# Perceiver layer on one core: the turned contexts of the cross-attention loop move behind the first score block, into the two value banks

## What is computed

```python
x = x + cross_attention(layernorm(x), ctx_768)      # 64 batches, 32 queries, 257 keys of 384, 16 heads of 64
x = x + self_attention(layernorm(x))                # 16 heads, a bias by relative position
x = x + ffn(layernorm(x))                           # weights and activations rounded to 8 bits; gated, 1408 wide
# cross_attention:
q, k, v = hidden @ Wq, ctx @ Wk, ctx @ Wv           # heads of 64
probs = softmax(q @ k.T / 8)
out = (probs @ v) @ Wo + bo
```

## Time and profile before

| | us |
|---|---|
| median of 3 runs | 1572.41 |
| lowest and highest | 1572.11, 1574.92 |
| the profiled execution, its own time | 1571.98 |
| its span, first to last instruction | 1570.2 |

### The profile page before, as it was taken

One profiled execution on the slowest core, in us unless ns is written; L12 is line 12 of the kernel. 1 busy time (PEld: TensorE's weight loads), 2 busy tenths in 40 slices (PEclk: granted clock), 3 DMA queues, 4 the chain that ended last, 5 costly groups with the idle time before them and its releaser, 6 DMA issues.

```text
span 1570.2 us, 36060 instructions
## 1 busy us (share of the span) xinstructions
PE 1533.9 (98%) x13794; PEld 1286.7 (82%) x13802; DVE 1063.5 (68%) x2274; ACT 736.5 (47%) x1596; POOL 371.4 (24%) x225
## 2 busy tenths in 40 slices
PE   7999989999999999999999999999999999998989
PEld 6888788899999899988989999888888888886544
DVE  8766677677667766677667767657555664556788
ACT  5444655555545554555455554433223222224755
POOL 1000234343444344443534344400000000000000
PEclk9999999999999999999999999999999999999999
DMA  6799863341433233332344143250220311323022
GB/s 239 317 369 355 316 254 126 140 146 52 140 136 141 68 116 139 139 109 75 139 139 144 53 140 124 82 195 29 94 83 29 122 42 42 115 77 128 1 107 107
DMA packets 78958, 210.74 MB, mean 134 GB/s; under 512 B 5712, under 2 KB 31760, under 8 KB 76048
## 3 DMA queue, kind: packets, MB, share of 16 engines
q1 hardware_dynamic: 78864, 209.39, 37.1%
HBM read 140.42 MB, written 68.94 MB: 133 GB/s over the span
## 4 chain that ended last, share of the span: by engine, by line
PE 89%; issue 6%; DVE 3%; ACT 1%; DMA 0%; SPq 0%; POOLq 0%; POOL 0%
PE psum_o L697 17%; PE psum_s L674 8%; PE psum_q L674 8%; PE psum_q L1538 6%; PE psum_o L1494 6%; PE psum_q L1494 6%; PE psum_q L727 6%; PE psum_t L1570 6%; PE psum_o L562 5%; PE psum_o L712 5%; PE psum_t L685 3%; PE psum_t L643 3%; PE psum_t L594 1%; PE psum_q L594 1%; PE psum_s L1525 1%
## 5 line engine op out<-in xcount | busy, mean ns | idle before, releaser
L697 PE MATMUL psum_o<-pT,c_nat 128*128 128x512 f32 x1152 | 307.4, 403 | 3.4 <-issue 2.4
L697 PEld LDWEIGHTS psum_o<-pT,c_nat 128*128 128x128 f32 x1152 | 204.6, 189 | 40.1 <-DVE pT L962 3.6
L1310 POOL TENSOR_TENSOR c_nat<-c_raw,constants 128x768 fp32r<-128x768 f32 x64 | 93.9, 1467 | 555.3 <-PE psum_o L697 440.7
L1163 DVE TENSOR_SCALAR oT<-psum_o,c_last 128x512 f32<-128x512 f32 x192 | 143.8, 749 | 66.5 <-PE psum_o L697 66.5
L889 ACT ACTIVATE probs<-psum_s,nmax 128x257 f32<-128x257 f32 x128 | 61.1, 477 | 233.0 <-DVE nmax L1178 233.0
L674 PE MATMUL psum_s<-cT,qk 128*128 128x256 f32 (+1 forms) x1152 | 163.8, 287 | 0.5 <-DVE cT L962 0.3
L674 PEld LDWEIGHTS psum_s<-cT,qk 128*128 128x128 f32 x1152 | 150.1, 189 | 6.6 <-issue 0.5
L674 PE MATMUL psum_q<-cT,qk 128*128 128x256 f32 (+1 forms) x1152 | 151.7, 283 | 1.0 <-DVE qk L1097 1.0
L674 PEld LDWEIGHTS psum_q<-cT,qk 128*128 128x128 f32 x1152 | 142.2, 189 | 4.0 <-issue 2.6
L962 DVE TENSOR_TENSOR pT<-psum_t,pT 128x512 fp32r<-128x512 f32 x128 | 87.8, 687 | 71.0 <-ACT pT L780 71.0
L1295 POOL TENSOR_TENSOR c_raw<-c_raw,last_row 128x768 f32<-128x768 f32 x64 | 120.3, 1880 | 29.6 <-DMA last_row<-in_ctx_dram 19.2
(11 more groups left out here) (295 smaller groups left out, 3114.5 us busy)
## 6 DMA issues: line engine op xcount, KB each, us to landing
qk_by_tile<-staged SPq DMA_DIRECT2D x32, 1536.0 KB, 10.2
raw<-qk_by_tile SPq DMA_DIRECT2D x16, 3072.0 KB, 12.6
c_raw<-in_ctx_dram SPq DMA_DIRECT2D x64, 384.0 KB, 3.2
last_row<-in_ctx_dram SPq DMA_DIRECT2D x64, 192.0 KB, 4.4
out_dram<-x_out SPq DMA_DIRECT2D x32, 256.0 KB, 2.0
x_res<-in_x_dram SPq DMA_DIRECT2D x16, 256.0 KB, 2.6
x_in<-out_dram SPq DMA_DIRECT2D x4, 1024.0 KB, 7.7
x_all<-out_dram SPq DMA_DIRECT2D x1, 4096.0 KB, 13.4
```

The lines of the kernel that those rows point to most:

```text
L697: i = pe.matmul(ps[:], c_nat[(b - 1) % 2][:, part, k, m * P:(m + 1) * P], pT[:, moving, k, :], start=(k, part, moving) == (0, 0, 0), stop= ...
L1163: nc.vector.tensor_scalar(oT[:, m, :, (b - 1) % 4, :], ps[:].rearrange("p (s q) -> p s q", q=SQ), c_last[:, (b - 1) % 2, m:m + 1], None, A ...
```

## The change

The six context transposes of a batch move from between the value blocks to a place behind S0, in between the probability transposes. The row is now: probabilities half 0 (t0), context chunk 2, probabilities half 1 (t1), context chunks 0 and 1 together. The contexts no longer go through t0 and t1 but through the banks of the coming PV0 and PV1. Chunks 0 and 1 share one bank, so that ScalarE and VectorE drain them with one instruction of 512 columns each. In b = 0 of the first tile all stays as it was. The tests of readiness are the same: probabilities by `s_scaled` and `s_normed`, contexts by `s_sub`. GpSimd's and SyncE's programs are untouched.

```diff
 def cross_units(section):
...
+        later = not (section == "last" and b == 3)
+        if b == 0 and section == "first":
+            u += [(("CT", b, c), ("t0", "t1")[c % 2]) for c in range(3)]
+            continue
+        u += turned_units(b)
+        if later:
+            u += [(("CT", b, 2), values_bank(b, 0)), (("CT", b, 0), values_bank(b, 1))]
         if b == 1 and section != "first":
             u += [(("W", 0), "o1"), (("W", 1), "o0")]
...
+        u += value_units(b)
         if b == 3 and section != "first":
             u.append((("WO",), "q1"))
-        if not (section == "last" and b == 3):
-            u += [(("CT", b, c), ("t0", "t1")[c % 2]) for c in range(3)]
...
         def pe_ctxT(pe, t, b, section, chunks):
 
-            if chunks[0] == 0:
+            if chunks[0] == chunks_of(b, section)[0][0]:
                 pe.wait_ge(s_sub, 4 * t + (b + 2))
-            for c in chunks:
-                pe_ctxT_chunk(pe, U1(("CT", b, c), t, section), c_raw[(b + 1) % 2], c)
+            pe_ctxT_chunk(pe, U1(("CT", b, chunks[0]), t, section), c_raw[(b + 1) % 2], chunks)
...
             for k in range(KI):
-                if k == KI // 2 and section in ("second", "loop"):
-                    pe_ctxT(pe, t, 3, section, (2,))
...
+                def turn():
+                    pe_probsT(pe, t, b, 0, section)
+                    if more or b < 3:
+                        pe_ctxT(pe, t, b, section, (2,))
+                    pe_probsT(pe, t, b, 1, section)
+                    if more or b < 3:
+                        pe_ctxT(pe, t, b, section, (0, 1))
+
                 pe_scores(pe, t, b, 0, section)
                 if before:
-                    pe_probsT(pe, t, b, section)
+                    turn()
                 pe_scores(pe, t, b, 1, section)
...
                 if before:
                     pe_pv(pe, t, b, 0, section)
-                if before and (more or b < 3):
-                    pe_ctxT(pe, t, b, section, (0, 1))
-                if before:
                     pe_pv(pe, t, b, 1, section)
                 if b == 3 and begun:
                     pe_wo(pe, t, section)
-                if before and (more or b < 3) and not (b == 3 and begun):
-                    pe_ctxT(pe, t, b, section, (2,))
                 if before:
                     pe_pv(pe, t, b, 2, section)
...
                 for k in range(2):
                     act_probsT(act, t, b, k, section)
+                    if after:
+                        ctxT(b, ((2,), (0, 1))[k])
...
                 row_max(b, 1)
+                if after:
+                    ctxT(b, (2,))
                 dve_probsT(dve, t, b, 1, section)
                 inverse(b, 0)
...
                 row_max(b, 2)
+                if after:
+                    ctxT(b, (0, 1))
                 inverse(b, 1)
```

More of the change, by code:

```diff
@@ L59, in project_units, with values_bank, turned_units, value_units @@
     return u
[L62 to L65 removed]
+def values_bank(b, m):
+    return ("o0", "o1")[(b * 3 + m) % 2]
+def turned_units(b):
+    return [(("PT", b, 0), "t0"), (("PT", b, 1), "t1")]
+def value_units(b):
+    return [(("PV", b, m), values_bank(b, m)) for m in range(3)]
 def cross_units(section):
@@ L502, in build_kernel @@
         NONE = {b: 0 for b in BANKS}
+        units, per = numbered(cross_units("loop"))
+        TURNED_LAST = {c: (units[("CT", 3, c)][0], units[("CT", 3, c)][1] - per[units[("CT", 3, c)][0]]) for c in (0, 2)}
+        units, per = numbered(cross_units("first"))
+        assert TURNED_LAST == {c: (units[("CT", 3, c)][0], units[("CT", 3, c)][1] - per[units[("CT", 3, c)][0]]) for c in (0, 2)}
         U1 = Stage(NONE, PLAN1)
@@ L676, in pe_scores, with pe_probsT @@
             m.then_inc(done, 1)
-        def pe_probsT(pe, t, b, section):
+        def pe_probsT(pe, t, b, k, section):
             pe.wait_ge(s_scaled, 8 * t + 2 * b)
             pe.wait_ge(s_normed, 8 * t + 2 * b)
[L682 to L686, removed]
+            ps, done = empty(pe, U1(("PT", b, k), t, section))
+            for rg in range(4):
+                m = pe.transpose(ps[:, rg * P:(rg + 1) * P], probs[(b - 1) % 2][:, rg, k * P:(k + 1) * P], ident[:])
+            m.then_inc(done, 1)
         def pe_pv(pe, t, b, m, section):
@@ L704, in pe_wv @@
                 pe.wait_ge(s_wvo, 32)
-                for m in range(KC):
-                    taken(pe, U1(("PV", 0, m), t, section))
+                taken(pe, U1(("PV", 0, KC - 1), t, section))
             ps, done = empty(pe, U1(("W", n), t, section))
@@ L762, in pe_cross_tail @@
             t, section = TILES, "tail"
-            pe_probsT(pe, t, 0, section)
+            for k in range(2):
+                pe_probsT(pe, t, 0, k, section)
             pe_self_x(pe, 0, (0, 1))
@@ L1187, in norm, with ctxT @@
                                         ALU.mult).then_inc(s_normed, 1)
-            def ctxT(b, c):
-                v = cT[(b + 1) % 2]
-                dve_cross_low(dve, ("CT", b, c), t, section, v[:, 1, c, 0:2 * P], v[:, 0, c, 0:2 * P], 2 * P)
+            def ctxT(b, chunks):
+                v, c, n = cT[(b + 1) % 2], chunks[0], len(chunks)
+                place, split = (f(("CT", b, c), t, section) for f in (U1, SPLIT1))
+                dve_low(dve, place, split, v[:, 1, c:c + n, 0:2 * P], v[:, 0, c:c + n, 0:2 * P],
+                        lambda ps: ps[:, 0:n * 2 * P].rearrange("p (c n) -> p c n", c=n))
             if not begun:
```

66 lines of the change are left out of this document (29 added, 37 removed).

## The result

| | before | changed |
|---|---|---|
| median, us | 1572.26 (1571.32 to 1574.92, 4 runs) | 1935.23 (1934.11 to 1936.64, 4 runs) |
| span of the profiled execution, us | 1570.2 | 1932.3 |
| mean granted TensorE clock | 0.995 | 0.917 |

The account below looks back on a forecast made before the run. TensorE, busy 98% of the span, was taken to bound the kernel. To 1571.98 us came +244.9 waits, +6.4 seam, +99.6 clock and -0.6 merging, 1922.3; forecast 1922 us, 22% slower, range 1865 to 1985.

Parts of the forecast that it names:

- What bounds: Whole loop: TensorE, busy 98% of the span; less VectorE or ScalarE work saves nothing, any TensorE wait adds in full.
- The transposes in one row: TensorE's transposes per batch: one row of 14 costs nearly the same as three short ones; 0.01 x 60 batches, -0.6 us.
- The wait: Moved context transposes: TensorE stands from T + 1.50 to T + 5.65 for GpSimd's subtraction, 4.15 us per batch, +244.9 us.
- The count of batches: Batches that pay the stall: 59, with none charged for the first tile's b = 0 and b = 1.
- The seam: Between first and second tile: PV0 at T + 26.7 instead of T + 19.6, costing +6.4 us.
- The clock: TensorE behind each stall: one half-clock stretch, 1.66 us for each of 60, +99.6 us, bounds 0 to 202.
- rival (B): Clock stays down two stretches behind most stalls: up to 2025 us, or some 1985 if at half of them; chance 0.12.
- What could be late next: VectorE and ScalarE work behind S1, value projection and PV0: 0 us taken, at worst 1.5 us kept for the range.
- Rival (C): Contexts ready in time, subtraction made by T + 1.5; rows merge and only returns count, 1561 to 1571 us; chance 0.05.
- an idle VectorE: Sign at the stall: much other than 4.15 us would mean GpSimd's instructions run faster or slower beside an idle VectorE.

Follow-up runs that it names:

- the run with the clock held: Changed kernel with 30 added score-like matmuls ahead of the wait for the subtraction in each of 62 batches; 1822.81 us, ratio 1.1592.
- the turned order: Changed kernel with GpSimd's order turned round, the next batch's last-key subtraction ahead of this batch's split; 1589.39 us, ratio 1.0105.

## Why the prediction was right, and where it was off

**What bounds.** Right: fewer drains (2212 VectorE instructions for 2274) saved nothing, and each wait of TensorE was added in full.

**The transposes in one row.** Forecast -0.6 us for 60 batches, 0.01 each. A batch b = 2 without waits took 9.99 in place of 10.00 us, which agrees, though a hundredth is the step of the rows. A batch b = 3 gained 0.07, where the forecast had 0.01. Even so it is about 1 us over 14 tiles: the term was rightly small.

**The wait.** Forecast 4.15 us per batch, T + 1.50 to T + 5.65. Measured 4.06, T + 5.56. GpSimd's subtraction and second half took 1.80 us each in place of 1.85 (TensorE stands still beside them now, see the last section), which makes 0.1 of difference. In the run with the clock held, a tile of the loop takes 67.5 us for 51.05, 4.11 per batch. The forecast of all waits with the seam was 250.7 us. Measured are 245.9, or 247.6 when the half-clock stretch that the kernel before has in this part, and that run has not, is counted back at 1.7. The whole times (1822.81 - 1572.68 = 250.1) agree better with 250.7 by luck: about 5 us of them are the added matmuls' own. The count of batches was right: 61 waits, of which the one at the seam is 4.95.

**The seam.** Forecast: PV0 of the second tile 26.7 us behind the last S0 row of the first tile, without the clock's share. It starts at 253.49, S0 at 223.23, 30.3 us; two stretches of half clock lie in it, 3.6 us over. In the run with the clock held it is 25.6 us (227.42 to 253.02), so without the clock the forecast was 1.1 too long, and the clock's share is 4.7. In the changed kernel's timeline the 4.95 us wait is where it was placed:

```profile
223.23 1.25 PE L697 MATMUL psum_s<-cT,qk 128*128 128x258 f32 x9
...
246.94 0.69 PE L656 MATMUL psum_o<-ident,c_raw 128*128 128x128 f32 x2 [4.95 <-POOL c_raw L1314]
...
253.49 4.36 PE L719 MATMUL psum_o<-pT,c_nat 128*128 128x512 f32 x18
```

**The clock, the term that was mis-sized.** Forecast 1.66 us for each of 60 stalls, 99.6 us, net of the one stretch of before; measured 115.9 for 61 stalls, 1.90 each, or 114.2 net. The clock was priced 15 us too low and the waits 3 too high; the two together are the 12 us between the forecast's 1922.3 and the profiled execution's 1934.1. I took one stretch of 3.41 us behind each stall. The changed kernel shows two kinds, nearly always in turn (length; busy; granted clock):

```profile
787.59:789.34 1.75, 0.00 (x0) 0.50 0.30 35
789.34:794.42 5.08, 5.08 (x24) 0.50 0.30 104
773.94:777.35 3.41, 3.41 (x19) 0.50 1.13 302
```

Behind the stall up to 773.62 the clock is halved for 3.41 us, all of them work. Around the next one it is halved from 787.59 to 794.42, 6.83 us, of which 1.75 fall into the idle time and cost nothing, and 5.08 into work. So a pair of stalls has 8.49 us of work at half clock, 4.2 each, and not 3.41. Over all 61 stalls 31 have the short stretch and 30 the long one, 260 us of work at half clock; a microsecond of it cost 0.45 us, a little less than the 0.49 of the price that I had read (1.68 for 3.41). That was rival (B), true at half of the stalls. Its price for the long stretch was too high since it left out that a part of it lies in the stall itself, although the rows of before show that: there the half clock begins at 1439.35 and the idle time ends at 1440.07. Its figure for half the stalls was also added wrongly: 1822.7 + 30 x 3.36 + 30 x 1.66 is 1973, not 1985. The sentence of the Trainium skill (TensorE: Matmul & The Clock Gate, What's actually happening) that the ramp costs under 1% of a typical span does not hold in this kernel: 115.9 of 1572 us is 7%, because the clock is lost in each batch.

**What could be late next.** Right that next to nothing was: from the seam on, TensorE's attended-value row waits for VectorE 0.16 us once at the seam and 0.2 us once later, and the value projection (L733) never. In the turned order, without the long wait, the value banks do show: the context transposes of b = 0 wait for the bank of VectorE's last value piece, 8 times, 2.2 us in all.

**Rival (C)**, that the contexts are ready in time, is what the turned order makes true. It does not come out faster, not even by the 3 us that could be told: the merged row gives about 1 us, and the run is 17 us slower all the same, by waits that the subtraction's new place brings (for its load, for the value banks, and for a VectorE that it holds up).

## What to carry to other kernels

Before a step is moved forward, follow what it waits for back to the engine that produces it, and ask what that engine's first instruction of the round waits for. Here it was the last block of the same queue, so what the order leaves uncovered of the distance between the two (5.5 us, of which 1.5 were covered) was a price in each batch, and fuller rows or joined drains had little to set against it on an engine that was never idle. Price a new stall twice, by its length and by the half clock behind it: here the second was 47% of the first. When matmuls are put into a stall to measure the clock's share, look for places where they fill no stall.

## What the runs showed of the hardware that was not expected

Idle stretches of 2.01 and 2.02 us of TensorE, in the same loop, had different ends: one was followed by 3.41 us at half clock, the other by none. In the kernel before 2.44 and 2.47 us had differed likewise. A stall of 2 us is not safe for the clock, and its length alone does not tell.

GpSimd and VectorE held each other up. In the run with the kernel before and GpSimd's order turned, the subtraction ran from 803.16 to 805.30, and the `qk` low part that was to start at 804.24 ended at 806.92: as long after 805.30 as it takes alone (1.75) less 0.13. Both read two operands from SBUF. The Trainium skill (SBUF — State Buffer, Who interferes with whom) says that a VectorE tensor_tensor with both inputs in SBUF contends with GpSimd's reads, and that one of the two is then blocked whole. The trace agrees for VectorE, with 0.93 us added to 1.75; but the subtraction, which had begun first, took 2.14 us in place of 1.85 as well. VectorE's normalizations of probabilities were held in the same way (0.61 us became 1.76 in the rows above). So when GpSimd works counts as well as how long: by the rows above these collisions are nearly all of the 18 us that the turn costs in the kernel before. In the changed kernel with the turn the rows name waits for the load and for the value banks, and how these 17 us divide the runs do not settle.

GpSimd's own speed followed TensorE, not VectorE. Its subtraction took 1.85 us in the median before, beside a working TensorE and VectorE. Below are the changed kernel, where both stand still beside it; the run with matmuls in the idle time, where TensorE works and VectorE stands still; and the run with the subtraction between the halves, where TensorE stands still and VectorE works for 0.69 us of it (least, median, most in ns):

```profile
L1314 POOL TENSOR_TENSOR c_raw<-c_raw,last_row x64: 1791/1800/3892, 19.4 to 1334.8; 128x768 f32<-128x768 f32 x64
L1318 POOL TENSOR_TENSOR c_raw<-c_raw,last_row x64: 1815/1837/1856, 19.1 to 1226.1; 128x768 f32<-128x768 f32 x64
L1314 POOL TENSOR_TENSOR c_raw<-c_raw,last_row x64: 1799/1802/1849, 18.8 to 1139.9; 128x768 f32<-128x768 f32 x64
```

1.80 us with TensorE idle, 1.84 with it busy. The prediction had looked to an idle VectorE for this. Why TensorE's work should matter to GpSimd, the runs do not show.
